# Pieces of four early expert steps put in another order on TensorE and ScalarE, and their biases loaded as whole rows

## The reference

```python
x = layernorm(x + attention(x))                    # one head of 256, full, no mask
x = layernorm(x + cross_attention(x, ctx, mask))   # 16 heads of 16, 64 keys
x = layernorm(x + experts(x))                      # 16 experts, the 4 best of each token
# experts, for each token and each of its 4 experts e, with router share c_e:
hmid = gelu(x @ w1[e] + b1[e])                     # 256 -> 512
out += (hmid @ w2[e] + b2[e]) * c_e                # 512 -> 256
```

## Time and profile before

| | us |
|---|---|
| median of three runs | 591.85 |
| the runs shown | 588.79, 591.85, 2253.84 |
| the profiled execution's own time | 591.44 |
| its span (first to last instruction) | 589.7 |
| PE busy | 545.5 (93% of the span) |
| early steps on PE, from the first transpose to the last down product | 278.16 to 328.56 |

### The profile page before, as it was taken

One profiled execution on the slowest core, in us unless ns is written; L12 is line 12 of the kernel. 1 busy time (PEld: TensorE's weight loads), 2 busy tenths in 40 slices (PEclk: granted clock), 3 DMA queues, 4 the chain that ended last, 5 costly groups with the idle time before them and its releaser, 6 DMA issues.

```text
span 589.7 us, 14213 instructions
## 1 busy us (share of the span) xinstructions
PE 545.5 (93%) x4044; PEld 503.5 (85%) x4044; DVE 400.0 (68%) x898; ACT 320.1 (54%) x657; POOL 269.8 (46%) x255
## 2 busy tenths in 40 slices
PE   5999999999998979889698999999998999999874
PEld 4988998888987868777577899999998999999862
DVE  2646656655668757687352698778876887888665
ACT  2424333333345535445344678767876687777605
POOL 6650000000014645655545445565655665776723
PEclk9999999999999989999889999999999999999988
DMA  8699999980000312317658999999999989999586
GB/s 272 214 384 385 386 385 385 387 280 0 1 1 32 126 51 90 112 66 243 185 192 207 256 245 269 254 265 248 238 250 250 239 239 242 286 244 227 65 239 206
DMA packets 93663, 127.49 MB, mean 216 GB/s; under 512 B 8817, under 2 KB 64817, under 8 KB 93633
## 3 DMA queue, kind: packets, MB, share of 16 engines
q1 hardware_dynamic: 78432, 107.23, 54.9%
q0 software_dynamic: 14304, 19.67, 16.5%
q10 hardware_dynamic: 896, 0.23, 0.2%
HBM read 62.59 MB, written 64.52 MB: 216 GB/s over the span
## 4 chain that ended last, share of the span: by engine, by line
PE 50%; issue 14%; DMA 13%; ACT 8%; DVE 8%; another core or an unknown queue 2%; POOL 1%; ACTq 1%; DVEq 0%; POOLq 0%; SPq 0%
DMA expert_sum<-yb,home_row 12%; PE ps L396 9%; PE ps L398 8%; PE ps L397 8%; PE ps L969 3%; PE ps L1077 3%; PE ps L896 3%; ACT hf L1466 2%; ACT w_h L1457 2%; PE ps L932 2%; ACT h_h L1473 1%; PE ps L953 1%; PE ps L1091 1%; PE ps L961 1%
## 5 line engine op out<-in xcount | busy, mean ns | idle before, releaser
L703 POOL DMA_INDIRECT expert_sum<-yb,home_row x76 | 150.0, 1974 | 96.3 <-DVE home_row L1915 50.3
L396 PE MATMUL ps<-w_h,h_h 128*128 128x256 f32 x288 | 82.0, 285 | 4.7 <-DVE h_l L1901 4.0
L396 PE MATMUL ps<-gT_h,w_h 128*128 128x256 f32 x288 | 83.6, 290 | 2.0 <-ACT hf L1466 1.3
L397 PE MATMUL ps<-w_l,h_h 128*128 128x256 f32 x288 | 81.4, 283 | 0.0
L398 PE MATMUL ps<-w_h,h_l 128*128 128x256 f32 x288 | 81.4, 283 | 0.0
L398 PE MATMUL ps<-gT_h,w_l 128*128 128x256 f32 x288 | 80.6, 280 | 0.0
L397 PE MATMUL ps<-gT_l,w_h 128*128 128x256 f32 x288 | 80.5, 279 | 0.0
L649 POOL DMA_INDIRECT expert_rows<-x_all,idx x64 | 63.0, 985 | 33.5 <-issue 29.9
L633 POOL TENSOR_TENSOR rstd<-ve,mhalf 128x1 f32<-128x1 f32 x16 | 8.8, 551 | 116.1 <-DVE ve L1634 116.1
L396 PEld LDWEIGHTS ps<-w_h,h_h 128*128 128x128 f32 x288 | 54.5, 189 | 6.9 <-DVE h_l L1901 3.1
L1466 ACT ACTIVATE hf<-ps,b1s 128x256 f32<-128x256 f32 x140 | 55.1, 488 | 4.9 <-PE ps L398 4.6
(11 more groups left out here) (297 smaller groups left out, 1408.8 us busy)
## 6 DMA issues: line engine op xcount, KB each, us to landing
expert_rows<-zeros SPq DMA_DIRECT2D x32, 1152.0 KB, 14.4
w1f<-in_L_ffn_w SPq DMA_DIRECT2D x40, 512.0 KB
w2f<-in_L_ffn_w SPq DMA_DIRECT2D x40, 512.0 KB
xg<-expert_rows SPq DMA_DIRECT2D x40, 288.0 KB
expert_sum<-zeros SPq DMA_DIRECT2D x10, 256.0 KB, 9.8
x_all<-in_x SPq DMA_DIRECT2D x8, 256.0 KB, 8.1
expert_sum<-x_all SPq DMA_DIRECT2D x8, 256.0 KB
total<-expert_sum SPq DMA_DIRECT2D x4, 512.0 KB, 5.7
```

The costliest lines, as they stand in the source:

```text
L396: pe.matmul(o, ah, bh, start=first, stop=False)
L397: pe.matmul(o, ah, bl, start=False, stop=False)
L703: pool.indirect_dma_start(out=sums[p], out_offset=bass.IndirectOffsetOnAxis(ap=home_row1[:, t, c:c + 1] if early else home_row[:, p, c:c + ...
```

## The change

The order on TensorE and ScalarE becomes another, and the biases of the early steps come another way. What each piece computes is the same. `turn_table` is a name for the lines L1117 to L1121, `step_biases` for L1124 to L1128. Before, one DMA for each step wrote 512 single numbers to b1s1, over the partitions. Now SP loads the four steps' rows of b1, 2 KB each, to four partitions of a scratch tile, ahead of all other loads of the early steps; TensorE turns them with four transposes (`turn_biases`), and ScalarE copies the result to b1s1 and waits for it. TensorE's first `turn_early` waits for that copy.

```diff
 # SP
             experts = [early_expert(t) for t in range(EARLY_STEPS)]
+            for t in range(EARLY_STEPS):
+                sp.dma_start(b1e[t:t + 1], b1[ds(experts[t], 1), :]).then_inc(f_b1, 16)
             for t in range(2):
                 load_rows(t, t, early_place(t))
                 load_up(t, t, experts[t])
                 load_down(t, t, experts[t])
-            for t in range(EARLY_STEPS):
-                sp.dma_start(b1s1[:, t], b1_flat[ds(experts[t] * I, I)].rearrange("(j p) -> p j", p=P), allow_slow_non_contiguous=True).then_inc(f_b1, 16)
 # TensorE
             def turn_early(t, p, k):
                 pe.wait_ge(f_x[p], 16 * k + 16)
                 if t == 0:
-                    pe.wait_ge(cqc, done(NT - 1))
+                    pe.wait_ge(b1c, 1)
                 else:
                     pe.wait_ge(gth, done(t - 1))
+            def turn_biases():
+                pe.wait_ge(f_b1, 16 * EARLY_STEPS)
+                pe.wait_ge(cqc, done(NT - 1))
+                for j in range(KI):
+                    mm = pe.transpose(ps[:, 4, j * EARLY_STEPS:(j + 1) * EARLY_STEPS], b1e[:, j * P:(j + 1) * P], ident[0:EARLY_STEPS, 0:EARLY_STEPS])
+                mm.then_inc(b1t, 1)
+            turn_biases()
+            at(cturn_p, NT - 1)
             at(turn_early, 0)
-            at(cturn_p, NT - 1)
             at(turn_o, NT - 2)
             at(up_early, 0, 0)
             at(positions, NT - 3)
             at(project, NT - 2)
             at(cattend_first, NT - 1)
+            at(turn_early, 1)
             at(cattend_rest, NT - 1)
             at(up_early, 0, 1)
             at(turn_o, NT - 1)
-            at(turn_early, 1)
             at(up_early, 1, 0)
             at(positions, NT - 2)
             at(project, NT - 1)
             at(up_early, 1, 1)
+            at(turn_early, 2)
             at(down_early, 0, 0)
             at(positions, NT - 1)
             at(down_early, 0, 1)
-            at(turn_early, 2)
+            at(up_early, 2, 0)
+            at(turn_early, 3)
             at(down_early, 1, 0)
             at(down_early, 1, 1)
...
-            at(up_early, 2, 0)
+            turn_table()
             at(up_early, 2, 1)
...
-            at(turn_early, 3)
             at(up_early, 3, 0)
+            step_biases()
             at(up_early, 3, 1)
             at(down_early, 2, 0)
             at(down_early, 2, 1)
 # ScalarE
+            act.wait_ge(b1t, 1)
+            act.activation(b1s1[:].rearrange("p j t -> p (j t)"), ps[:, 4, 0:KI * EARLY_STEPS], ACT.Copy).then_inc(b1c, 1)
+            act.wait_ge(b1c, 1)
+            at(p_out, NT - 1)
             at(copy_early, 0)
-            at(p_out, NT - 1)
 ...
             at(x1_again, NT - 1)
+            at(copy_early, 1)
             at(o_out, NT - 1)
-            at(copy_early, 1)
 ...
             at(gelus_early, 1)
+            at(copy_early, 2)
 ...
             at(y_early, 0)
-            at(copy_early, 2)
+            at(copy_early, 3)
             at(y_early, 1)
             at(gelus_early, 2)
 ...
-            at(copy_early, 3)
+            at(gelus_early, 3)
             for half in range(2):
                 pack_shares(half)
-            at(gelus_early, 3)
             at(y_early, 2)
```

More of the change, by code:

```diff
@@ L154, in decoder_layer @@
     w2_rows = w2.rearrange("e h d -> (e h) d")
-    b1_flat = b1.rearrange("e h -> (e h)")
     with ExitStack() as stack:
@@ L343, in decoder_layer @@
         shift1 = sbl("shift1", [NSTEP, E])
-        b1s1 = sbl("b1s1", [P, EARLY_STEPS, KI])
+        b1s1 = sbl("b1s1", [P, KI, EARLY_STEPS])
         gT1 = sbl("gT1", [P, 2, KD, SLOT])
@@ L375, in decoder_layer @@
         lidx = count("lidx")
-        sc_early = sem("sc_early"); sc_late = sem("sc_late"); tb1 = sem("tb1"); f_b1 = sem("f_b1")
+        sc_early = sem("sc_early"); sc_late = sem("sc_late"); tb1 = sem("tb1"); f_b1 = sem("f_b1"); b1t = sem("b1t"); b1c = sem("b1c")
         tb = sem("tb"); tb_ps = sem("tb_ps"); tb_dve = sem("tb_dve"); b1_ok = sem("b1_ok")
@@ L411, in store_tiles @@
             q.dma_start(half[a * P:(a + size) * P, :].rearrange("(a p) d -> p a d", p=P), src[:, a:a + size, 0:D]).then_inc(ld_sum, 16)
+        b1e = shT[0:EARLY_STEPS].rearrange("p a c -> p (a c)")
         block = stack.enter_context(nc.Block())
@@ L1093, in down_early, with turn_table, step_biases @@
                     mm.then_inc(yps, 1)
+            def turn_biases():
[4 more added lines that the diff above has]
+                mm.then_inc(b1t, 1)
+            def turn_table():
+                pe.wait_ge(tb_dve, TABLE_STEPS)
+                pe.wait_ge(lgb, done(NT - 1))
+                pe.wait_ge(x2, done(NT - 1))
+                pe.transpose(ps[0:2, 7, 0:NSTEP], tabf[:], ident[0:NSTEP, 0:NSTEP])
+                pe.transpose(ps[0:E, 7, NSTEP:2 * NSTEP], stepe[:], ident[0:NSTEP, 0:NSTEP]).then_inc(tb_ps, 1)
+            def step_biases():
+                pe.wait_ge(ld_c, 16 * 7)
+                pe.wait_ge(tb, 2)
+                for j in range(KI):
+                    mm = pe.matmul(ps[:, 7, 2 * P + j * NSTEP:2 * P + (j + 1) * NSTEP], b1r[:, j * P:(j + 1) * P], stepeT[:], start=True, stop=True)
+                mm.then_inc(tb_ps, 1)
+            turn_biases()
+            at(cturn_p, NT - 1)
             at(turn_early, 0)
-            at(cturn_p, NT - 1)
             at(turn_o, NT - 2)
@@ L1112, in _ @@
             at(down_early, 0, 1)
-            at(turn_early, 2)
+            at(up_early, 2, 0)
+            at(turn_early, 3)
             at(down_early, 1, 0)
             at(down_early, 1, 1)
[L1117 to L1121, removed]
-            at(up_early, 2, 0)
-            at(up_early, 2, 1)
[L1124 to L1128, removed]
-            at(turn_early, 3)
+            turn_table()
+            at(up_early, 2, 1)
             at(up_early, 3, 0)
+            step_biases()
             at(up_early, 3, 1)
@@ L1376, in gelus_early @@
                 act.wait_ge(yps, freed(t))
-                act.wait_ge(f_b1, 16 * EARLY_STEPS)
                 for j in range(KI):
                     ins = act.activation(hf[:, p, j], ps[:, 2 * p + j // 2, (j % 2) * SLOT:(j % 2 + 1) * SLOT],
-                                         ACT.Gelu, bias=b1s1[:, t, j:j + 1])
+                                         ACT.Gelu, bias=b1s1[:, j, t:t + 1])
                 ins.then_inc(gel, 1)
```

## The result

| | before | after |
|---|---|---|
| median | 590.08 us (22 runs) | 585.11 us (22 runs) |
| range | 584.99 to 2253.84 | 579.73 to 591.80 |
| profiled execution, its span | 591.44, 589.7 | 587.42, 585.6 |

The ratio is 0.9934, with a 95% interval of 0.9911 to 0.9957: 3.9 us faster (2.5 to 5.3), within the 2% called no change. The two medians are 4.97 us apart, which lies inside that interval. The forecast was 4.8 us.

What follows compares the result with a forecast made beforehand. PE, busy 93% of the span, was taken as the bound, with waits in the early steps. Waits 3.42 + clock 1.7 - table 0.3 = 4.8 us, so 591.4 became 586.6; range 583.5 to 591.5.

Steps and rivals of the forecast that it cites:

- The fixed point: VectorE's wait before turn_o of tile 15: ends with GpSimd's send burst at 290.26, whatever the order on PE.
- Ahead of the gap: Before turn_o of tile 15: PE arrives about 1.5 us later, at no cost while the 3.73 us idle time covers it.
- the bias rows: SP's four row loads ahead of the early steps' loads: 2.4 us (bounds 1.6 and 5.6), hidden; removing old loads gives nothing.
- At the gap: Behind turn_o of tile 15: step 1's up product starts 1.18 us earlier, 0.49 of transposes and 0.69 of waiting.
- After it: Waits before step 1's down product, the table and step 3's up product go: 0.68, 0.80, 0.76 us; step 3's down wait stays.
- The clock: Low clock stretch after turn_o of tile 15 ends after 3.41 us, at 295.28: gain 1.7 us, bounds 0 and 3.1.
- rival 1: Low clock stretch as long as before because another wait falls in it: gain 3.1 us, 588.3; chance 0.2.
- the upper bound of 3.1: Most the clock could give in the early steps, in us, with no drop at all behind turn_o of tile 15.
- The table just in time: Before the table's transposes: table ready at 308.4, PE there at 308.7 to 308.9; 0.3 us taken off.
- rival 3: Loop of later steps gives the gain back, paced by loads and scatters: 591.4; chance 0.13.
- rival 4: Hand-over to ScalarE's bias copy at `turn_early(0)` is late: 0.8 us slower, 592.2; chance 0.07.
- Rival 2: No low clock stretch behind turn_o, as PE's gap shrinks to some 2.3 us: gain 6.2 us, 585.2; chance 0.12.

Runs made afterwards that it cites:

- chip 13: Set of runs where the kernel before took 568.61 us: six sends held with the table later 570.07, kernel before again 568.77, changed kernel again 565.57.
- filled kernel: Changed kernel plus six thrown-away products on PE between step 0's last up product and turn_o of tile 15: 584.27 us, ratio 0.9923.

## Why the prediction was right

It held in sign, range and about in size, with one term wrong. That the size is near is luck in part: the clock's term was 1.6 us too large, and against it 0.3 us was taken off for a table that was not late, and some 0.6 us was not counted.

- **The fixed point.** "They come when the burst is over" holds for VectorE's division near 590 us, but not as a rule. In the profiles of the changed kernel and of the four variants with all eight sends together it stands 1.04 to 1.13 us behind the last send. In the kernels with four sends held it is 1.04 to 1.18 us behind the fourth, but there its product itself ended only 0.5 to 0.9 us after that send, so 0.2 to 0.5 us of lateness is all that can show. Against the rule stands ScalarE's copy of step 1 in the changed kernel, 1.80 us before the last send's end, and the first profile, where the division came 0.45 us ahead of it. I take the latter for a chance of that execution: the kernel with the bias rows alone has the old order and 1.04, but no second profile of the kernel before near 590 us shows it. The point was not fixed at 290.26 either: turn_o came at 294.61 after 4.87 us of idle time, where 291.2 and 2.3 were forecast. This cost the forecast nothing, since the waits behind turn_o were won all the same. Held sends show the cause, and plain work of GpSimd shows that its being busy is not it. What in the sends does it, and why the kernels on chip 13 were free of it, stays open.
- **Ahead of the gap, and the bias rows.** Costed at nothing under the cover of the idle time, and 1.0 us without it. The four small transposes are a row of 0.41 us (279.39), behind which the next row starts after 0.33; 0.5 was forecast. SP's first load of rows went out 3.65 us after the first bias row (276.07 and 272.42), not 2.4, within the bounds, and no wait for them shows on PE. In the kernel with the rows alone PE waited 0.64 us more for ScalarE's copy of the biases, and the ratio was 0.9989. Right; and on chip 13, where nothing covers it, 0.62 + 0.33 us of it showed.
- **At the gap, 1.18 us.** Measured: 1.14 between turn_o and the up product, 0.98 in the stage when it is undone.
- **After it, 0.68 + 0.76 + 0.80.** All three brackets are gone, the last 0.69 stayed as forecast. With the gap's 1.14 that is 3.38; the stage shows 4.12 between the two first profiles, 3.74 between the rows-only kernel and the changed one. Of the 0.74 us more, 0.13 is the low stretch (5.86 us of work in it in place of 6.13). I put the other 0.6 to the rows beside the brackets: when nothing is waited for, a row starts up to 0.16 us before the one ahead of it ends (308.67 + 0.60 against 309.11), so a bracket of 0.68 is worth more than it shows. That is an estimate.
- **The clock, 1.7 us.** This is the step that failed. The prediction had the clock fall 0.69 us after turn_o, as before, and then, PE being busy throughout, rise after 3.41 us. But the stretch began while PE was still idle (0.97 us before turn_o), and lasted 6.83 us as before; in the variants with the burst left whole and no filler it was the same. The term was worth 0.13 us in place of 1.7. The sum without the term is 3.1, rival 1's number, and 3.9 was measured; rival 1 had the length right for another reason, a further wait inside the stretch, which is not there. The whole stretch is worth 2.87 us in the filled kernel's profile, so the upper bound of 3.1 was well placed.
- **The table just in time, 0.3 off.** No bracket before it in the changed kernel. With the sends held it was the next to be late, by 1.14.
- **Rivals.** The loop gave nothing back (rival 3). The new hand-over (rival 4) showed as a wait of at most 0.64 us. Rival 2, no low stretch, is what the changed kernel's profile on chip 13 shows, where the idle time before turn_o is not there either.

## What to carry to other kernels

When two short chains are woven by hand into one engine's list, put each copy out of PSUM behind a piece of another chain: the brackets of 0.7 us went when this was done and came back when it was undone (the table's, which is no copy, only in part). Before you price an idle time, see in the trace when the semaphore came, not only when the producer's row ended: the largest wait of this stage belonged to a third engine. And a fix that rests on such a lateness should be run where the lateness is absent, for six sends held, with the table later, cost 5 us there.

## What the runs showed of the hardware

PE's updates reached VectorE up to 5.8 us and ScalarE up to 5.2 us after the end of the product's row while GpSimd issued indirect DMAs back to back; in the one profile with plain work on GpSimd in their place they did not. In one set of runs, on another chip, this was absent and the kernel before was 21 us shorter; the change won the same there.

PE's clock does not follow from the length of the last idle time alone. After 2.33 us it stayed up once, and after 3.73 and 4.87 us it fell for 6.82 and 6.83 us. But it also fell after 1.91 us (for 3.41, the kernel before with held sends) and 2.60 us (for 3.42, six sends held), and in the kernel before on chip 13 for 3.41 us where no idle time of the 14 us ahead was over 0.76.
